# A ranking network on one core: which engine fetches embedding rows, and who copies the weights' high parts

## The reference

```python
B, F, E, H = ids.shape[0], 26, 64, 125000     # 2048 rows of ids, 26 fields
D = F * E                                      # 1664
x0 = emb[ids].reshape(B, D)
x = x0
for i in range(3):
    s = x @ cross_w[i]
    x = x0 * s[:, None] + cross_b[i] + x
h = relu(x0 @ w1 + b1)                         # 1664 -> 1024
h = relu(h @ w2 + b2)                          # -> 512
h = relu(h @ w3 + b3)                          # -> 256
out = sigmoid(concat([x, h], axis=1) @ out_w + out_b)
```

## Time and profile before

| | us |
|---|---|
| median of 3 runs | 538.0 |
| lowest, highest | 537.65, 539.04 |
| the profiled execution | 539.25 |
| its span | 537.4 |

### The profile page before, as it was taken

One profiled execution on the slowest core, in us unless ns is written; L12 is line 12 of the kernel. 1 busy time (PEld: TensorE's weight loads), 2 busy tenths in 40 slices (PEclk: granted clock), 3 DMA queues, 4 the chain that ended last, 5 costly groups with the idle time before them and its releaser, 6 DMA issues.

```text
span 537.4 us, 11277 instructions
## 1 busy us (share of the span) xinstructions
PE 470.0 (87%) x2876; PEld 436.3 (81%) x2876; DVE 184.4 (34%) x383; ACT 104.9 (20%) x194; POOL 379.4 (71%) x407
## 2 busy tenths in 40 slices
PE   0078599999899999999898998989899897999997
PEld 0078489898898889788897988889798887988996
DVE  4464522414242331424232241423223142322325
ACT  6595511101110110111111020111111011101111
POOL 5777557577777777777777777777777777777720
PEclk9998999999999999999999999999999999999999
DMA  8992111011111111111111111111111111111100
GB/s 231 224 363 81 24 23 26 22 30 26 30 28 29 27 29 29 29 27 30 28 29 25 30 30 28 27 29 28 27 29 27 30 26 29 28 28 26 28 10 2
DMA packets 19700, 24.90 MB, mean 46 GB/s; under 512 B 9305, under 2 KB 10292, under 8 KB 19636
## 3 DMA queue, kind: packets, MB, share of 16 engines
q0 software_dynamic: 12800, 13.13, 11.9%
q1 hardware_dynamic: 4770, 10.74, 5.7%
q10 hardware_dynamic: 2066, 0.31, 0.3%
HBM read 24.41 MB, written 0.01 MB: 45 GB/s over the span
## 4 chain that ended last, share of the span: by engine, by line
PE 52%; ACTq 12%; POOL 10%; issue 9%; ACT 6%; DMA 6%; DVE 5%; POOLq 0%; DVEq 0%
PE l_bank L716 40%; ACTq L390 11%; POOL x_raw L342 10%; DMA x_raw<-in_L_rec_emb,idx 5%; PE x_bank L716 4%; PE x_bank L732 4%; PE h_bank L760 3%; ACT xT_hi L403 2%; ACT w_hi L360 2%; DVE x_raw L521 2%; ACTq L387 1%; DVE xT_lo L528 1%; PE l_bank L791 1%; ACT h_bank L370 1%; DVE h2T_lo L533 1%
## 5 line engine op out<-in xcount | busy, mean ns | idle before, releaser
L342 POOL DMA_INDIRECT x_raw<-in_L_rec_emb,idx x400 | 378.5, 946 | 134.0 <-issue 107.2
L716 PE MATMUL l_bank<-w_hi,xT_hi 128*128 128x342 f32 (+1 forms) x624 | 145.6, 333 | 10.1 <-DVE xT_lo L528 10.1
L716 PE MATMUL l_bank<-w_hi,xT_lo 128*128 128x342 f32 (+1 forms) x624 | 138.4, 322 | 0.0
L716 PE MATMUL l_bank<-w_lo,xT_hi 128*128 128x342 f32 (+1 forms) x624 | 137.9, 321 | 0.0
L716 PEld LDWEIGHTS l_bank<-w_hi,xT_hi 128*128 128x128 f32 x624 | 104.0, 191 | 15.0 <-DVE xT_lo L528 13.6
L716 PEld LDWEIGHTS l_bank<-w_hi,xT_lo 128*128 128x128 f32 x624 | 106.9, 191 | 0.0
L716 PEld LDWEIGHTS l_bank<-w_lo,xT_hi 128*128 128x128 f32 x624 | 106.8, 190 | 0.0
L528 DVE TENSOR_TENSOR xT_lo<-x_bank,xT_hi 128x512 fp32r<-128x512 f32 (+1 forms) x66 | 38.2, 578 | 168.8 <-ACT xT_hi L403 168.8
L403 ACT ACTIVATE xT_hi<-x_bank 128x512 fp32r<-128x512 f32 (+1 forms) x66 | 33.5, 507 | 261.8 <-PE x_bank L732 205.4
L732 PE MATMUL x_bank<-identity,x_raw 128*128 128x128 f32 x208 | 34.8, 280 | 44.0 <-DVE x_raw L521 26.9
L732 PEld LDWEIGHTS x_bank<-identity,x_raw 128*128 128x128 f32 x208 | 25.2, 142 | 52.6 <-issue 49.9
(11 more groups left out here) (90 smaller groups left out, 289.5 us busy)
## 6 DMA issues: line engine op xcount, KB each, us to landing
ids<-in_L_rec_emb SPq DMA_DIRECT2D x1152, 0.2 KB
ids<-in_L_rec_emb ACTq DMA_DIRECT2D x896, 0.2 KB
w_raw<-in_L_rec_w SPq DMA_DIRECT2D x18, 512.0 KB, 21.7
x_raw<-in_L_rec_emb,idx POOLq DMA_INDIRECT x400, 2.4
b_rows<-in_L_rec_b SPq DMA_DIRECT2D x1, 512.0 KB
b_rows<-in_L_rec_b SPq DMA_DIRECT2D x1, 256.0 KB
ids<-in_r_ids SPq DMA_DIRECT2D x1, 208.0 KB, 2.7
b_rows<-in_L_rec_b SPq DMA_DIRECT2D x1, 128.0 KB
```

The costliest lines, as they stand in the source:

```text
L342: pool.indirect_dma_start(out=dst, out_offset=None, in_=emb, in_offset=rows).then_inc(landed, 16)
L716: done = pe.matmul(bank[:, 0:b - a], x[:, k, :], w[:, k, a:b], start=(k == 0 and n == 0), stop=(k == last_k and n == 2))
```

## The change

Fields and tiles: SyncE fetches field 24 in all tiles from 2 on (14), ScalarE field 23 (instead of 25) in ten tiles, with larger shares; GpSimd has 392 gathers. The rows' byte addresses come in the order of `AT_ROWS`. A `fetch` that finds all rows fetched returns. In tile 0 the indices of the fields from the third on (`QUICK`) use the low bits, so tile 0's first group too gets its predicated copy, and the indices come in three parts. The copies of the weights' high parts to PSUM are matmuls by an identity on TensorE (`copy_hi`), five of them ahead of tile 0's first transposes, two after, and one after each chunk of layer 1; ScalarE only rounds. There are no late pieces any more, and VectorE's order in the first step is written out.

```diff
-    SP_TILES = [2, 4, 6, 8, 9, 10, 12, 14, 15]
+    SP_TILES = list(range(2, TILES))
-    ACT_TILES = [3, 5, 7, 9, 11, 13, 15]
-    ACT_FIELD = F - 1
+    ACT_TILES = [3, 4, 5, 7, 8, 9, 11, 12, 13, 15]
+    ACT_FIELD = F - 3
-    ACT_SHARES = [8, 12, 4, 16, 12, 12]
+    ACT_SHARES = [12, 20, 4, 28, 16, 16]
+    QUICK = 2
+    ONE_RUNS = [(SP_FIELD, 2, 1), (ACT_FIELD, 3, 4), (ACT_FIELD, 4, 4), (ACT_FIELD, 5, 4)]
+    AT_ROWS = [(f, t) for f, a, every in ONE_RUNS for t in range(a, TILES, every)]
-    SPLITS = [range(0, 6), range(6, 10), range(10, 13), range(13, 15)]
-    LATE = range(15, len(LOADS))
+    HI_AHEAD = [range(0, 6), range(6, 12), range(12, 16), range(16, len(LOADS))]
+    COPIES = 5
+    COPY_WITH = 7
+    LO_WHOLE = [4, 9, 12, 16]
+    LO_READ = [5, 10, 13, 17]
+        identity_r = sb("identity_r", [P, P], F32R)
...
             def split_hi(n):
                 raw, hi, _ = parts(n)
                 act.wait_ge(weights_loaded[n], 16)
                 act.activation(hi, raw, ACT.Copy).then_inc(hi_split, 1)
-                act.wait_ge(hi_split, n + 1)
-                if n == LATE[0]:
-                    act.wait_ge(h1T_ready, 2)
-                for i in range(2):
-                    bank, free_at = bank_of(n, i)
-                    if free_at > 0:
-                        act.wait_ge(weights_split, free_at)
-                    half = half_of(hi, i)
-                    act.activation(like(bank, half), half.bitcast(F32), ACT.Copy).then_inc(hi_staged, 1)
...
             def fetch(share):
                 j, p = fetched[0] // P, fetched[0] % P
+                if j == len(ACT_TILES):
+                    return
+                assert p + share <= P
                 if p == 0 and j >= ACT_BUFS:
                     act.wait_ge(act_placed, j - ACT_BUFS + 1)
-                row = len(SP_TILES) + j
+                row = AT_ROWS.index((ACT_FIELD, ACT_TILES[j]))
...
             def first_step():                      # VectorE
+                split = 0
                 for g in range(NG):
-                    for n in SPLITS[g]:
+                    for n in range(split, LO_WHOLE[g]):
                         split_lo(n)
+                        if n == 0:
+                            dve.wait_ge(end_row_loaded, 16)
+                            link(dve.tensor_copy(end_bank, end_row[:, :]))
+                    make_whole(0, g)
+                    for n in range(LO_WHOLE[g], LO_READ[g]):
+                        split_lo(n)
+                    x_lo(0, g)
+                    split = LO_READ[g]
                     if g == 0:
                         cross_consts()
-                        dve.wait_ge(end_row_loaded, 16)
-                        link(dve.tensor_copy(end_bank, end_row[:, :]))
-                    x_lo(0, g)
-                    if g < NG - 1:
-                        make_whole(0, g + 1)
+                for n in range(split, len(LOADS)):
+                    split_lo(n)
...
             dve.wait_ge(ids_loaded, 16)
-            to_indices(0, FIRST)
+            to_indices(0, QUICK)
+            to_indices(QUICK, FIRST)
             to_indices(FIRST, TILES * F)
...
+            def copy_hi(n):                        # TensorE
+                if n >= len(LOADS):
+                    return
+                pe.wait_ge(hi_split, n + 1)
+                for i in range(2):
+                    bank, free_at = bank_of(n, i)
+                    if free_at > 0:
+                        pe.wait_ge(weights_split, free_at)
+                    half = half_of(parts(n)[1], i)
+                    pe.matmul(bank[:, 0:HALF], identity_r[:, :], half.rearrange("p m c -> p (m c)"),
+                              start=True, stop=True).then_inc(hi_staged, 1)
...
             def first_step():                      # TensorE
+                for n in range(COPIES):
+                    copy_hi(n)
                 transpose_x(0, 0)
+                for n in range(COPIES, COPY_WITH):
+                    copy_hi(n)
                 for g in range(NG):
                     l1(0, g, BODY, first=True)     # copy_hi(k + COPY_WITH) after each chunk k
```

More of the change, by code:

```diff
@@ L50, in dcn_ranker_kernel @@
     assert SP_FIELD // FPK in GROUPS[-1] and SP_FIELD // FPK in LAST_GROUPS[3]
-    ACT_TILES = [3, 5, 7, 9, 11, 13, 15]
-    ACT_FIELD = F - 1
+    ACT_TILES = [3, 4, 5, 7, 8, 9, 11, 12, 13, 15]
+    ACT_FIELD = F - 3
     ACT_BUFS = 2
-    ACT_SHARES = [8, 12, 4, 16, 12, 12]
+    ACT_SHARES = [12, 20, 4, 28, 16, 16]
     assert ACT_FIELD // FPK in GROUPS[-1] and all(
-        sum(ACT_SHARES) * (t - 1) >= P * (j + 1) for j, t in enumerate(ACT_TILES)) and P % sum(ACT_SHARES) == 0
+        sum(ACT_SHARES) * (t - 1) >= P * (j + 1) for j, t in enumerate(ACT_TILES))
+    ONE_RUNS = [(SP_FIELD, 2, 1), (ACT_FIELD, 3, 4), (ACT_FIELD, 4, 4), (ACT_FIELD, 5, 4)]
+    AT_ROWS = [(f, t) for f, a, every in ONE_RUNS for t in range(a, TILES, every)]
+    assert sorted(AT_ROWS) == sorted([(SP_FIELD, t) for t in SP_TILES] + [(ACT_FIELD, t) for t in ACT_TILES])
     ROW = E * 4
@@ L95, in dcn_ranker_kernel @@
     LOADS += [("w3", k, W3K) for k in range(0, K3, W3K)]
-    SPLITS = [range(0, 6), range(6, 10), range(10, 13), range(13, 15)]
-    LATE = range(15, len(LOADS))
-    assert all(GROUPS[g][-1] < SPLITS[g].stop for g in range(NG))
+    HI_AHEAD = [range(0, 6), range(6, 12), range(12, 16), range(16, len(LOADS))]
[3 more added lines that the diff above has]
+    LO_READ = [5, 10, 13, 17]
+    assert all(HI_AHEAD[g].stop > max(COPIES - 1, GROUPS[g][0] - 1 + COPY_WITH - 1) for g in range(NG))
     ctx = ExitStack()
@@ L288, in _ @@
                     regs = [sync.alloc_register(f"sp_row{i}_{p + j}") for j in range(SP_REGS)]
-                    sync.load(regs, at_bytes[at_row[t]:at_row[t] + 1, p:p + SP_REGS])
+                    row = AT_ROWS.index((SP_FIELD, t))
+                    sync.load(regs, at_bytes[row:row + 1, p:p + SP_REGS])
                     for j, reg in enumerate(regs):
@@ L331, in _ @@
                     for f in fields(ks):
+                        if t == 0 and f == QUICK:
+                            pool.wait_ge(idx_ready, 2)
                         if t == 0 and f == GROUPS[-1][0] * FPK:
@@ L430, in first_step @@
                 for g in range(NG):
-                    for n in SPLITS[g]:
+                    for n in HI_AHEAD[g]:
                         split_hi(n)
@@ L687, in _ @@
             dve.wait_ge(ids_loaded, 16)
-            to_indices(0, FIRST)
+            to_indices(0, QUICK)
+            to_indices(QUICK, FIRST)
             to_indices(FIRST, TILES * F)
-            dve.wait_ge(idx_ready, 2)
+            link(dve.tensor_scalar(past[:, 0:QUICK], ids[:, 0:QUICK], float(H), None, ALU.is_ge))
+            dve.wait_ge(idx_ready, 3)
             copied = 0
[L692 to L695, removed]
+            for field, first, every in ONE_RUNS:
+                tiles = range(first, TILES, every)
                 a, b = (t * F + field for t in (tiles[0], tiles[-1]))
@@ L723, in transpose_x @@
                 ks = groups(t)[g]
[L724 to L728, removed]
+                pe.wait_ge(x_whole, NG * t + g + 1)
                 if g == 0 and t > 1:
@@ L753, in l1 @@
                             three_passes([(l1_bank[i], a, b)], xT_hi, xT_lo, w1_hi, w1_lo, k, last).then_inc(l1_done, 1)
+                    if first:
+                        copy_hi(k + COPY_WITH)
             def h1_chunks(t, bank, ks):
```

23 lines of the change are left out of this document (9 added, 14 removed).

## The result

The changed kernel takes 550.19 us (median of 4 runs, 549.48 to 553.04; the profiled one is the longest of them) against 538.49: ratio 1.0225, 95% interval 1.0191 to 1.026.

A forecast was written before the change was run, and what follows sets the result against it. ScalarE's in-order queue was taken to decide, with SyncE, GpSimd and TensorE near the same period: h1 eviction at 51, 13 steps of 41.2, step 14 at 34.5, 41.8 to the end, clock 3.9: 667 us, range 645 to 690.

The forecast's parts named there:

- the price of a row: Each row fetch in ScalarE's queue costs 0.36 us, bounds 0.33 and 0.42, taken from the kernel of before.
- the prediction's sum: ScalarE's stretches between evictions, with 96 rows, add up to 41.2 us a step in steps 1 to 13, against 30.8.
- The prediction's own signs of being wrong: Evictions in steps 1 to 13 still waiting for TensorE, row pitch below 0.3, or SyncE or GpSimd setting the period.
- The rival of the other side: ScalarE's fetches cost the path nothing; SyncE's and GpSimd's fetches set the end: 523 us, chance 0.05.
- The forecast's picture: In each step evictions queue behind ScalarE's row bursts, and TensorE gets two long holes, about 4 and 5 us.
- Group 1's stretch at 2.5 us: From h2's eviction to group 1's, with 4 rows, ScalarE's stretch stays unchanged at 2.5 us.
- 0.3 us a step for the clock: TensorE's slow clock after the second hole costs 0.3 us a step, 0 at the low end, 2 at the high.
- SyncE's 33 us a tile: SyncE's row fetches take 32.9 us for each tile of 128 rows, over 14 tiles.
- From step 14's h1 eviction to the end: The last stretch, bound by TensorE with no fetch in it, takes 41.8 us.
- Tile 0: Eighth gather lands at 19 to 20, layer 1 starts at 22.6, h1 eviction at 51, 6 us earlier, bounds 48 and 57.
- the start's gain would vanish in step 1: Late chunks removed after tile 0's h1 eviction gain nothing, as ScalarE's own queue sets step 1's length.
- Step 14: With only two shares left, 12 and 20 rows, this step takes 34.5 us.

The follow-up runs named there:

- e1: The changed kernel with ScalarE fetching field 25, whose rows lie inside the table, in place of field 23: 674.75 us.
- e10: The kernel of before with the two fields swapped, SyncE fetching field 25 and ScalarE field 24: 536.37 us.
- e5: The changed kernel with shares 16, 16, 8, 20, 16, 20, a share that crosses tiles issued in two parts: 520.04 us.
- e6: The changed kernel with the first two shares swapped, 20, 12, 4, 28, 16, 16: 545.4 us.
- e7: The changed kernel with shares 12, 20, 4, 20, 20, 20, so 20 rows instead of 28 ahead of group 2's eviction: 529.37 us.
- e9: The changed kernel with ScalarE's field and all tiles and shares of before, and seven of tile 0's first eight fields clamped again: 535.4 us.

## Why the prediction was wrong

**The step that failed** is the price of a row: "0.36 us a row", with bounds of 0.33 and 0.42, carried from field 25 over to field 23. The price belonged to the rows, not to the engine. Field 25's ids lie inside the table and each of its DMAs moves 256 bytes. Of field 23's, seven in eight are past it; the address that the kernel computes for them lies beyond the table, and the DMA is skipped by its bounds check (`bounds_check="skip_entire_dma"` in the kernel). Issues in the changed kernel, ScalarE and SyncE:

```profile
L395 ACTq DMA_DIRECT2D ids<-in_L_rec_emb x1280: 90/90/515, 54.9 to 490.8; - x183
...
L300 SPq DMA_DIRECT2D ids<-in_L_rec_emb x1792: 73/73/313, 31.4 to 494.3; - x200
```

In the step shown the bursts of 96 rows take 19.8 us together (the burst of 4, not shown, 0.64). By the prediction's own reckoning, in which 6.68 - 16 x 0.36 = 0.92 us of the stretch from group 1 to group 2 are not rows, that stretch is 7.9 us on average over steps 1 to 13 and leaves (7.9 - 0.92)/28 = 0.25 us a row, not 0.36. e1 and e10 show that it is the ids by changing the fields alone.

**What the price alone doesn't give.** With 0.25 the prediction's sum would be 41.2 - 96 x 0.11 = 30.6 us a step, no loss at all, and the steps were 32.8 on average. The sum took the step for one full queue. With cheap rows the queue isn't full: the stretches with room end when TensorE is ready, and only the bursts that are longer than TensorE's work beside them cost something. Mean stretches between evictions over steps 1 to 13, us:

| stretch (rows) | predicted | e1, rows moved | changed kernel |
|---|---|---|---|
| h1 to group 0 (12) | 6.0 | 5.4 | 5.2 |
| group 0 to h2 (20) | 8.3 | 8.5 | 5.6 |
| h2 to group 1 (4) | 2.5 | 2.9 | 2.5 |
| group 1 to 2 (28) | 11.0 | 11.5 | 7.9 |
| group 2 to 3 (16) | 6.7 | 7.2 | 5.7 |
| group 3 to h1 (16) | 6.7 | 6.8 | 5.9 |
| step | 41.2 | 42.2 | 32.8 |

**It could have been read.** The trace of before and the inputs held it. The median issue was 0.235 us on ScalarE and 0.073 on SyncE, a factor of three between two engines that issue the same instruction:

```profile
L292 SPq DMA_DIRECT2D ids<-in_L_rec_emb x1152: 73/73/318, 40.2 to 364.9; - x192
```

The prediction gives the first figure alone and calls SyncE's "the same kind of row". And the ids say which: 25 fields reach a million (fields 23 and 24 among them), the last one, field 25, stays below 124,982. The diff changed the field, and the sum did not ask what else that changed. The prediction's own signs of being wrong came: a pitch of rows below 0.3 (28 rows in 5.50 us are 0.20), and evictions that still wait for TensorE.

**The rival of the other side** named the right point, 0.27 us a row, below which SyncE's period would decide, and dismissed it on the issue's 0.234, the same wrong figure. Its time, 523 us, is e5's (520.04) within 3: but only with other shares. With the change's own, what it left out decided: at 0.25 us a row the 96 rows fit in the step, and two of its bursts still don't fit where they stand. The forecast's picture holds there at a smaller size: evictions late behind their bursts, two holes a step, TensorE's clock falling after some.

**What held.** Group 1's stretch at 2.5 us. The 41.2 us a step for rows that are moved: 42.2 on average in e1. Some 0.35 of the missing 1.0 us is the stretch from h2 to group 1, with transposes at a lower clock; the rest lies in the stretches around groups 2 and 3, partly in ScalarE's own queue, and was not taken apart. So 0.3 us a step for the clock was small at least. In e1 the clock over the whole run was 0.91, in the kernel of before 0.99, with holes of 4.70 and 4.25 us in one of its steps. The Trainium skill (TensorE: Matmul & The Clock Gate, section "Loop structure matters more than you think") says that a loop with a long wait for a DMA between its matmuls lets TensorE go cold. Here the wait was for ScalarE's queue, and e1's trace agrees in direction. SyncE's 33 us a tile held too, since its field 24 stayed the same (462.97/14 = 33.1 in e5). From step 14's h1 eviction to the end it took 42.1 us, predicted were 41.8.

**Tile 0.** The first predicated copy, which waits for the eight gathers, started at 18.99 (landing at 19 to 20 was expected). Layer 1 began at 24.88, not 22.6: on the way TensorE's copies waited 0.78 us for ScalarE and 0.98 for VectorE. The h1 eviction came at 53.3, not 51.

**What else was off**: that the start's gain would vanish in step 1. It is 8.9 us by tile 1's h1 eviction, because ScalarE's queue was no longer the bound; in e1, where it is, that eviction comes at 95.40, later than before. Step 14 took 29.2 us, not 34.5.

## What to carry to other kernels

A price read off a row belongs to that row's data too: when a change moves an operation to other indices or addresses, ask whether the measured instances were of the same kind, and take two engines that differ threefold at one instruction as a question. Work slipped into an in-order queue has to fit each gap between the instructions that others wait for, not only the step's total: the same 96 rows cost 550 or 520 us by how they are shared out. Judge each gap by itself: here the two late ones were nearly independent, in spans 7.7 us were won at the one (e6), 22.4 at the other (e7) and 33.8 at both (e5), and the larger was the one that vanished whole and took the slow clock with it. Even a right price in a sum over the step would have shown none of it.

## What the hardware showed beyond what was expected

A skipped DMA still costs its issuer 0.073 us on SyncE and 0.090 on ScalarE, about a third of one that moves 256 bytes (0.228 and 0.235). Seven gathers of mostly one and the same row held everything that the DMA engines moved beside them, the weights above all, to 201 GB/s at a DMA share of 0.98, where spread rows let 355 through at 1.02 (e9 and the changed kernel, 10 to 24 us).
